# Scores and key maxima of an attention kernel in one PSUM block: two tiles and 256 columns at a time

## The reference, cut to what matters

```python
q, k, v = heads(query @ Wq.T + bq), heads(bank @ Wk.T + bk), heads(bank @ Wv.T + bv)   # 16 heads of 16
scores = einsum('bhqd,bhkd->bhqk', q / sqrt(16), k)      # 64 queries, 1601 keys per batch
attn = softmax(scores, axis=-1)
ctx = einsum('bhqk,bhkd->bhqd', attn, v)                 # then @ Wo.T + bo
```

## Time and profile before

| what | value |
|---|---|
| median of 3 runs | 2128.44 us (2126.26 to 2132.22) |
| the profiled execution | 2133.82 us, its span 2132.0 us |
| mean granted TensorE clock | 0.984 of full speed |
| PE busy | 1976.3 us, 93% of the span |
| DVE busy | 1314.6 us, 62% |
| ACT busy | 1049.9 us, 49% |
| POOL busy | 614.4 us, 29% |
| DMA | 112 GB/s read and written over the span |

### The profile page before, as it was taken

How to read it: one execution, slowest core, us unless ns; L and a number is a source line. 1 busy time by engine, 2 the same in 40 slices (tenths; PEclk the granted TensorE clock), 3 DMA queues, 4 the chain that set the end, 5 groups by cost and what they waited for, 6 DMA issues and landing times.

```text
span 2132.0 us, 72414 instructions
## 1 busy us (share of the span) xinstructions
PE 1976.3 (93%) x31796; PEld 1590.1 (75%) x31796; DVE 1314.6 (62%) x2276; ACT 1049.9 (49%) x1532; POOL 614.4 (29%) x997
## 2 busy tenths in 40 slices
PE   5798999999999999999999989999999998999987
PEld 4577777777778787787778778787787776778764
DVE  2557656856666566666666576665666666566644
ACT  3455445555455555555555544555544444444441
POOL 3322323323233232323323232332323222122201
PEclk8999999999999999999999999999999999999999
DMA  5533434243333333424333324242342321213122
GB/s 184 182 125 119 145 117 138 102 135 128 121 117 114 122 132 117 146 91 159 112 129 124 123 93 162 77 158 90 120 135 85 119 70 61 77 52 105 49 71 69
DMA packets 124469, 243.90 MB, mean 114 GB/s; under 512 B 13952, under 2 KB 44800, under 8 KB 124160
## 3 DMA queue, kind: packets, MB, share of 16 engines
q1 hardware_dynamic: 123568, 239.23, 34.0%
q10 hardware_dynamic: 592, 0.04, 0.0%
HBM read 235.94 MB, written 3.15 MB: 112 GB/s over the span
## 4 chain that ended last, share of the span: by engine, by line
PE 73%; DVE 12%; ACT 7%; issue 5%; POOL 2%; DMA 0%; SPq 0%; POOLq 0%; DVEq 0%; ACTq 0%
PE M L805 11%; PE M L812 11%; PE SC L1023 9%; PE SC L1046 8%; PE O L1067 7%; PE X L862 5%; ACT probT L1269 4%; DVE mx L1612 4%; PE SC L1039 3%; PE M L862 3%; PE X L1133 2%; PE X L1107 1%; PE M L867 1%; PE X L841 1%; PE M L906 1%
## 5 line engine op out<-in xcount | busy, mean ns | idle before, releaser
L1612 DVE TENSOR_REDUCE mx<-SC 128x4 f32<-128x1600 f32 (+1 forms) x256 | 466.8, 1823 | 145.2 <-PE SC L1023 142.1
L1269 ACT ACTIVATE probT<-SC 128x2048 f32<-128x2048 f32 (+1 forms) x256 | 398.8, 1558 | 165.4 <-PE SC L1046 164.9
L654 POOL TENSOR_TENSOR rowsT<-raw,rowsT 128x384 fp32r<-128x384 f32 (+1 forms) x256 | 279.6, 1113 | 394.4 <-ACT rowsT L1323 394.2
L812 PE MATMUL M<-wvs,rowsT 128*128 128x256 f32 x2496 | 358.6, 293 | 2.3 <-ACT kT L1208 1.4
L805 PE MATMUL M<-rowsT,wks 128*128 128x400 f32 (+1 forms) x1536 | 342.7, 364 | 11.6 <-DVE V L1414 4.8
L1208 ACT ACTIVATE kT<-M,bk 128x400 f32<-128x400 f32 (+1 forms) x256 | 151.5, 593 | 382.8 <-PE M L805 382.4
L805 PEld LDWEIGHTS M<-rowsT,wks 128*128 128x128 f32 x1536 | 271.8, 191 | 86.2 <-issue 64.4
L812 PEld LDWEIGHTS M<-wvs,rowsT 128*128 128x128 f32 x2496 | 315.1, 192 | 22.6 <-issue 2.5
L1414 DVE TENSOR_TENSOR V<-M,bv 128x512 f32<-128x512 f32 (+1 forms) x224 | 145.3, 649 | 278.0 <-PE M L812 269.8
L1023 PE MATMUL SC<-kT,bdq 32*128 32x400 f32 (+1 forms) x2048 | 244.9, 546 | 27.7 <-ACT probT L1269 23.0
L1067 PEld LDWEIGHTS O<-probT,V 128*17 128x17 f32 x13312 | 195.0, 99 | 79.7 <-issue 75.2
(11 more groups left out here) (275 smaller groups left out, 2461.3 us busy)
## 6 DMA issues: line engine op xcount, KB each, us to landing
ring<-in_ws_dram SPq DMA_DIRECT2D x428, 256.0 KB, 4.6
summed<-in_ctx_dram SPq DMA_DIRECT2D x60, 800.5 KB, 4.6
raw<-in_ctx_dram SPq DMA_DIRECT2D x64, 384.0 KB, 4.5
raw<-in_ctx_dram SPq DMA_DIRECT2D x32, 512.0 KB, 4.0
ring<-rounded_scratch SPq DMA_DIRECT2D x64, 256.0 KB, 4.0
raw<-in_ctx_dram SPq DMA_DIRECT2D x32, 321.0 KB, 4.7
out_dram<-x SPq DMA_DIRECT2D x16, 128.0 KB, 2.2
kT<-in_ctx_dram SPq DMA_DIRECT2D x2, 800.5 KB, 8.9
```

The lines of the kernel that those rows point to most:

```text
L654: pool.tensor_tensor(rowsT[1][:, c, at], raw[:, c, at], rowsT[0][:, c, at], ALU.subtract).then_inc(low_ready, 1)
L812: mm = pe.matmul(bank[:, (t - 2 * a) * D:(t - 2 * a + 1) * D], rowsT[xp][:, cc, t * P:(t + 1) * P], wvs[wp][:, cc, :], start=(at == cc == ...
L1269: act.activation(probT[step % 3][0:w, :, 0:len(ts), :].rearrange("p j t q -> p j (t q)"), SC[0:w, :, 0:len(ts) * P], ACT.Exp)\
L1612: dve.tensor_reduce(mx[c][:, :, n], SC[:, :, 0:KCH[n][1]], AX.X, ALU.max).then_inc(max_used, 1)
```

## The change

The banks of `SC` are halved: columns 0 to 255 hold scores of two key tiles, columns 256 to 511 the scores of 256 keys for the maxima. Both are filled in one visit, a **block**, with one semaphore (`block_filled`). ACT then takes the exponential of the left half, and after it DVE reduces the right half; the next block starts after both. A half of a batch takes 7 blocks: slots 0, 1 and 2 (and 4, 5, 6) have two, one at the slot's start and one where the maxima were, slots 3 and 7 have one. The maxima run 10 blocks ahead. In slots 1 and 5 the second block holds the last chunk of maxima, of 65 keys. In DVE's order the reduction of the slot's first block stands ahead of the drains of "first" pieces. The key chunks become 512, 512, 256 and 321 wide (`KCH`), the pieces of the split 4, 4, 2 and 3 tiles (`PIECES`, before 4, 3, 3, 3).

```diff
-NCH = (KEYS + 511) // 512
-KCH = [(KEYS * n // NCH, KEYS * (n + 1) // NCH - KEYS * n // NCH) for n in range(NCH)]
+KCH = [(lo * P, min(hi * P, KEYS) - lo * P) for lo, hi in ((0, 4), (4, 8), (8, 10), (10, KT))]
+HALF = 2 * P
+HALVES = (KEYS + HALF - 1) // HALF
-LEAD = 6
+BLOCKS = C * HALVES
+LEAD = 10
-FIRST_WARM = (1, 2, 3, 4)
+FIRST_WARM = (2, 4, 6, 8)
-PIECES = [(0, 4, key(1, 1)), (4, 7, key(1, 2)), (7, 10, value(4)), (10, KT, value(VF - 1))]
+PIECES = [(0, 4, (key(1, 0), value(1))), (4, 8, (value(2),)), (8, 10, (value(4),)), (10, KT, (value(VF - 1),))]
...
+def halves(k):
+    return 1 if k % NTG == NTG - 1 else 2
+def block_at(b, k, h):
+    i = BLOCKS * b + k // NTG * HALVES + 2 * (k % NTG) + h
+    return i, i + LEAD
+def half_tiles(k, h):
+    lo = 4 * (k % NTG) + 2 * h
+    return range(lo, min(lo + 2, KT))
+def max_chunk(j):
+    mb, n = divmod(j, BLOCKS)
+    c, n = divmod(n, HALVES)
+    return mb, c, n, n * HALF, min(KEYS - n * HALF, HALF)
...
+                def scores_and_maxima(b, k, h):
+                    i, j = block_at(b, k, h)
+                    if j < 0 or i >= BLOCKS * B:
+                        return
+                    if j in FIRST_WARM:
+                        warm(2)
+                    if j:
+                        pe.wait_ge(max_used, min(j, BLOCKS * B))
+                    if i > 0:
+                        pe.wait_ge(exp_ready, i)
+                    if i >= 0:
+                        mm = scores(b, k, h)
+                    if j < BLOCKS * B:
+                        mm = maxima(j)
+                    mm.then_inc(block_filled, 1)
...
                 for b, k in SLOTS:
-                    if 0 <= b < B:
-                        scores(b, k)
+                    scores_and_maxima(b, k, 0)
...
-                    maxima(b, k)
+                    if halves(k) > 1:
+                        scores_and_maxima(b, k, 1)
...
-                def exps(b, k):
+                def exps(b, k, h):
...
-                    act.wait_ge(score_filled, step + 1)
-                    if step >= 3:
+                    act.wait_ge(block_filled, j + 1)
+                    if h == 0 and step >= 3:
                         act.wait_ge(weighed, weighings(step - 3))
...
-                def maxima(b, k):
+                def maxima(b, k, h):
...
-                    dve.wait_ge(max_filled, s + 1)
-                    dve.tensor_reduce(mx[c][:, :, n], SC[:, :, 0:KCH[n][1]], AX.X, ALU.max).then_inc(max_used, 1)
+                    dve.wait_ge(block_filled, j + 1)
+                    if j >= LEAD:
+                        dve.wait_ge(exp_ready, j - LEAD + 1)
+                    dve.tensor_reduce(mx[c][:, :, n], SC[:, :, HALF:HALF + kn], AX.X, ALU.max).then_inc(max_used, 1)
...
+                    maxima(b, k, 0)
                     for what in pieces(b, k, "first"):
                         drain(what)
...
-                    maxima(b, k)
+                    if halves(k) > 1:
+                        maxima(b, k, 1)
```

More of the change, by code:

```diff
@@ L384, in program @@
         wk, wv = (probT[n].rearrange("p a b q -> p (a b q)")[:, 0:C * D].rearrange("p (c f) -> p c f", c=C) for n in range(2))
-        mx = [sp.sb(f"mx{c}", [P, 4, NQ]) for c in range(C)]
+        mx = [sp.sb(f"mx{c}", [P, 4, HALVES]) for c in range(C)]
         nmx = [sp.sb(f"nmx{c}", [P, 4]) for c in range(C)]
@@ L1027, in scores, with maxima @@
-                def scores(b, k):
-                    c, g = k // NTG, k % NTG
-                    step = STEPS * b + k
-                    pe.wait_ge(max_used, min(STEPS * b + k + LEAD, STEPS * B))
-                    if step:
-                        pe.wait_ge(exp_ready, step)
-                    if g == 0:
-                        x_is_used(pe, f"max{c}", b)
-                    ts = list(tiles(g))
-                    for j in range(4):
-                        r = slice(32 * j, 32 * j + 32)
-                        w = held(ts[0])
-                        pe.matmul(SC[0:w, j, 0:len(ts) * P].rearrange("p (t q) -> p t q", q=P), sel[r, 0:w],
+                def maxima(j):
+                    mb, c, n, k0, kn = max_chunk(j)
+                    if n == c == 0:
+                        pe.wait_ge(bd_ready, mb + 1)
+                    for a, (lo, w) in enumerate(KCH):
+                        if lo <= k0 < lo + w:
+                            wait_drained(pe, (mb, "key", a, c))
+                    for q in range(4):
+                        r = slice(32 * q, 32 * q + 32)
+                        mm = pe.matmul(SC[:, q, HALF:HALF + kn], bdq[mb % 2][r, c, :, :].rearrange("p e q -> p (e q)"),
+                                       keys(mb, c)[r, k0:k0 + kn], start=True, stop=True, skip_group_check=True)
+                    return mm
@@ L1040, in scores @@
+                def scores(b, k, h):
+                    c = k // NTG
+                    if k % NTG == h == 0:
+                        x_is_used(pe, f"max{c}", b)
+                    ts = half_tiles(k, h)
+                    w = held(ts[0])
+                    for q in range(4):
+                        r = slice(32 * q, 32 * q + 32)
+                        pe.matmul(SC[0:w, q, 0:len(ts) * P].rearrange("p (t q) -> p t q", q=P), sel[r, 0:w],
                                   mT[b % 2][c][r, :].unsqueeze(1).to_broadcast([32, len(ts), P]),
@@ L1160, in _ @@
                         fill_x(what, b)
-                    if k in WEIGH_FIRST:
-                        weigh(*rounds_weighed(b, k))
-                    maxima(b, k)
+                    if halves(k) > 1:
+                        scores_and_maxima(b, k, 1)
                     for what in pieces(b, k, "strips"):
                         fill(what)
-                    if k not in WEIGH_FIRST:
-                        weigh(*rounds_weighed(b, k))
+                    weigh(*rounds_weighed(b, k))
                     for what in x_fills(b, k, "C"):
@@ L1260, in gates @@
                     return act.activation(v[:, h, :], halves[:, 0, :, :], ACT.Relu)
-                def exps(b, k):
+                def exps(b, k, h):
+                    if not 0 <= b < B:
+                        return
                     step = STEPS * b + k
-                    ts = list(tiles(k % NTG))
+                    i, j = block_at(b, k, h)
+                    ts = half_tiles(k, h)
                     w = held(ts[0])
-                    act.wait_ge(score_filled, step + 1)
-                    if step >= 3:
+                    act.wait_ge(block_filled, j + 1)
+                    if h == 0 and step >= 3:
                         act.wait_ge(weighed, weighings(step - 3))
-                    act.activation(probT[step % 3][0:w, :, 0:len(ts), :].rearrange("p j t q -> p j (t q)"), SC[0:w, :, 0:len(ts) * P], ACT.Exp)\
+                    act.activation(probT[step % 3][0:w, :, 2 * h:2 * h + len(ts), :].rearrange("p j t q -> p j (t q)"), SC[0:w, :, 0:len(ts) * P], ACT.Exp)\
                        .then_inc(exp_ready, 1)
@@ L1319, in high_part @@
                     if n:
-                        wait_filled(act, (n - 1, *what))
+                        for fill in what:
+                            wait_filled(act, (n - 1, *fill))
                     else:
```

57 lines of the change are left out of this document (17 added, 40 removed).

## The result

The changed kernel takes 2301.21 us (median of 4 runs, 2295.59 to 2307.51) against 2129.59 of the kernel before in the same series (2126.26 to 2132.22): a ratio of 1.0808, 95% interval 1.0773 to 1.0842. The forecast had the sign (slower, 0.74) and was far off in size: +62 us, with a range to 2245, for +171. In the profiled executions the spans are 2132.0 and 2297.1 us, 165 apart.

A forecast was written before the change was run, and what follows sets the result against it. PE was taken to stand between two bounds, its own work and the ring. The terms, -63 + 18 + 49 + 55 + 5 + 7 = +71, were taken as +62 on 2128.4: 2190 us, range 2110 to 2245.

The forecast's parts named there:

- the ring: One block's cycle of fill (1.17), exponential (1.02), reduction (1.21) and handoffs: 3.65 us a block.
- exposed loads: Rival: in each of 448 blocks the first maxima load waits for the scores, +45 to +85 us; chance 0.1.
- term 4: Clock falls behind PE's new pauses: a third of 31, half of it hidden, +7 us; bounds 0 and +43.
- term 1: The 64 one-block slots (3 and 7) lose the maxima visit and some key columns: 0.98 us each, -63 us.
- the key columns: Columns leaving slots 3 and 7 reappear in slots 0, 1, 4 and 5; half their cost charged, +18 us.
- term 2: The 192 two-block slots, where the ring bounds: 80 first gaps and 50 second ones pay, +49 us.
- term 3: DVE's list makes slot 1's first reduction late by 1.8 us in 31 batches: +55 us; other first blocks +5.
- terms 2 and 3 partly fall on the same slots: Overlap of ring and list losses in the same slots: the sum of +71 us was taken as +62.
- the clock falls often: Rival: every pause costs a low clock stretch, +36 us more, 2226 us; counted in the forecast's range, no separate chance.
- POOL, SP and the sizes of the context pieces ... nothing: They move the same columns with the same number of operations, POOL 29% busy: nothing charged.
- The first 10 blocks ... nothing: They run before any scores, over the same slots as the first 6 steps did: nothing charged.
- saved visits win: Rival: PE's work fills most gaps above 2.5 us, so the kernel gets faster, 2098 to 2113 us; chance 0.18.

The follow-up runs named there:

- vfirst: The changed kernel with DVE's drains of the first fills put back ahead of each block's first reduction: 2423.29 us, ratio 1.1380.
- before_keys: The kernel before with only the new key fills and context pieces, maxima keeping their chunks: 2118.34 us, ratio 0.9957.
- hold: The changed kernel with 14 matmuls that compute nothing ahead of PE's wait for slot 1's second block: 2286.24 us, ratio 1.0741.
- the crossed kernel: The changed kernel with each block's exponential and reduction cut in half by banks, ACT and DVE changing places: 2247.60 us, ratio 1.0541.

## Why the prediction was wrong

Right were the direction, the places and each length: the ring (3.65 forecast, 3.66 measured), the exponential, the reduction, the handoff from ACT to DVE (0.12 forecast, 0.09 at 251.6), no exposed loads, and slot 1 as the worst place. The rule of the Trainium skill that spoke for exposed loads (TensorE: Matmul & The Clock Gate, Part 3: Packing small matmuls) did not hold here: the maxima's loads at 1194.15 run under score matmuls of their own row groups, and none is exposed.

The sum failed in two steps above all: **term 4, the clock**, was mis-sized sixfold, and **the drain of values behind the reduction** was put at nothing. The forecast's terms beside the reckoning:

| us | forecast | measured (rise against before) |
|---|---|---|
| PE's own work (term 1 and the key columns) | -63 + 18 = -45 | -33 |
| ring (term 2): waits outside slot 1's second block | +49 | +60 |
| list (term 3): waits at slot 1's second block | +55, +5 | +57 |
| clock (term 4) | +7 | +45 |
| waits of other matmuls | nothing | +28 |
| ahead of the first scores, and tail | nothing | +8 |
| "terms 2 and 3 partly fall on the same slots" | -9 | none seen |
| sum | +62 | +165 |

- **Term 4** took a third of 31 pauses at one place, with half of it hidden. There are 30 low stretches instead of 9. Only 8 of them start in slot 1's second block; most of the others start in slots 0, 1, 2, 4 and 6. The upper bound, +43, was about what was measured, and the rival "the clock falls often" was right in this term.
- **The drain of values** is the term that is missing. The prediction named what waits behind DVE's list, but not what waits behind the reduction itself. PE's waits for a bank `M` behind that drain rose from 14 to 40 us, nearly all of the +28. `vfirst` shows the cause: with the drain ahead of the reduction, its largest line falls from 20.0 to 5.0 us, though the ring then loses far more. And with the reduction cut to 16 columns all waits of this kind are 13 us.
- **Term 1** was too large. Slots 3 and 7 were to be "shorter by about a microsecond". Their mean lengths (scores to the next slot's scores, batches 1 to 30) went from 7.53 and 7.33 to 6.98 and 6.98 us, 0.45 and not 0.98 on average. The key columns alone account for it: `before_keys` has 6.98 and 6.94. The visit's saving returned as waits.
- **Term 3** was about right: half of the list out of the way gave 36 us.
- **Term 2** came out 11 us above the forecast, partly by luck. It took its count from the gaps that waited before (80 and 50, each at a fixed price). But a longer ring also reaches gaps that didn't wait: 10 blocks are bound at 2.65 us, 60 at 3.15 and 109 at 3.65. What each of these waits costs beyond itself stands in the terms for the clock and the drain.
- **"+62 rather than +71"** went the wrong way. The two losses add: cutting the list pays 36 us with the long ring and 51 with the short one.
- **"POOL, SP and the sizes of the context pieces ... nothing"**: the new pieces and fills on the kernel before are 9 us faster, so no loss was missed here. **"The first 10 blocks ... nothing"**: the first scores start at 99.1 us, not at 90.8. Kernels with the same start have them between 94.3 (`hold`) and 99.1, and `before_keys` at 96.7; how much of these 8 us is the change stays open.

The rival "saved visits win" needed gaps longer than the ring; with a ring of 2.65 us the changed kernel does come under the one before (2111 against 2128), but not under it with its own maxima cut in the same way (2094).

What stays open: the split of the 165 us between clock and waits rests on the reckoning, since `hold` moves only one place and little time. I have no version in which all pauses stay and the clock doesn't fall. And how the 190 us of the cut reductions divide between the ring and DVE's queue is not measured; the crossed kernel only gives a hint.

## What to carry to other kernels

Merging two visits to a buffer saves an engine's work and puts the two consumers one behind the other; compare the new ring with the whole distribution of gaps, not with the gaps that wait today, since the price grew faster than the ring. Then price what the new pauses bring with them: here the waits for the ring and the list came out near the forecast, and the clock and a drain one place further back in the queue made most of the miss. A consumer in an in-order queue is as late as the list ahead of it and makes late whatever is behind it: before moving one, write down the due date on each side. If two consumers must share banks, cross them by halves, and cut long lists in front of them: here that took back 105 of 171 us (2301 to 2196), though not the whole.

## What was not expected of the hardware

- The clock follows short pauses in an engine that is otherwise busy: behind a pause of 2.89 us at 1199.8 the same 16 score records took 0.95 us for 0.62, and the granted clock of the eight microseconds around was 0.79. Shortly ahead of 27 of the changed kernel's 30 low stretches, or at their start, PE had stood still once for 1.4 to 4.1 us. The crossed kernel has fewer waits than the changed one (85 before blocks for 189), and still more time at 1.2 GHz (160 us for 133).
- The reduction from PSUM costs 223 ns for 64 elements, 723 for 544 and 1223 for 1024, so 1.04 ns an element over some 156 ns. Cut in two by banks, the reductions of the 448 blocks keep DVE busy for 539.5 us and not 497.0, the exponentials ACT for 496.5 and not 431.8: crossing costs DVE 0.09 and ACT 0.14 us a block, and shortens the ring by 0.94.
